# Attention over 64 graphs in even steps of one unit each, its probabilities transposed by DMA instead of TensorE

## What is computed

```
B, N, D, H = 64 graphs, 128 nodes, 512, 8 heads of 64
def attn(q, k, v, mask):
    scores = einsum('bhid,bhjd->bhij', q, k) * 64 ** -0.5
    w = softmax(where(mask > 0, scores, -inf))
    return einsum('bhij,bhjd->bhid', w, v)
edges = ln(attn(x @ wq1, x @ wk1, x @ wv1, adj.T) + x)          # pass 0
nodes = ln(attn(x @ wq2, edges @ wk2, edges @ wv2, adj) + x)    # pass 1
h = gelu(nodes @ w1 + b1)
out = layernorm(x + ln(nodes + h @ w2 + b2))
```

## Time and profile before

| | |
|---|---|
| time, median of 3 runs | 3141.88 us (3140.71 to 3142.14) |
| profiled execution, first to last instruction (span) | 3138.1 us |
| PE busy | 3028.9 us, 97% of the span |
| DVE, ACT, POOL busy | 56%, 45%, 48% of the span |
| DMA moved | 228.50 MB, mean 73 GB/s |
| TensorE clock granted, mean | 0.995 |

### The profile page before, as it was taken

One profiled execution on the slowest core, in us unless ns is written; L12 is line 12 of the kernel. 1 busy time (PEld: TensorE's weight loads), 2 busy tenths in 40 slices (PEclk: granted clock), 3 DMA queues, 4 the chain that ended last, 5 costly groups with the idle time before them and its releaser, 6 DMA issues.

```text
span 3138.1 us, 54583 instructions
## 1 busy us (share of the span) xinstructions
PE 3028.9 (97%) x18944; PEld 2511.9 (80%) x18944; DVE 1765.9 (56%) x4762; ACT 1422.4 (45%) x3754; POOL 1507.8 (48%) x1418
## 2 busy tenths in 40 slices
PE   8999999999899999999998999999999999999996
PEld 7888888888788888878887888888888888888885
DVE  6777777777787878777776233333232333332334
ACT  5656565656566666566665322222222222222221
POOL 3656564656466667676764233333323333332324
PEclk9999999999999999999999999999999999999998
DMA  4121212221223233333334311101111111001101
GB/s 155 59 74 60 71 61 71 64 75 59 81 92 115 98 114 99 112 101 111 100 108 134 99 54 54 43 18 53 53 47 53 53 53 53 27 33 53 54 34 60
DMA packets 167312, 228.50 MB, mean 73 GB/s; under 512 B 7168, under 2 KB 72832, under 8 KB 167168
## 3 DMA queue, kind: packets, MB, share of 16 engines
q1 hardware_dynamic: 167168, 226.86, 22.2%
HBM read 159.73 MB, written 67.11 MB: 72 GB/s over the span
## 4 chain that ended last, share of the span: by engine, by line
PE 84%; DVE 11%; issue 2%; ACT 2%; DMA 1%; SPq 0%; DVEq 0%; POOL 0%; POOLq 0%; ACTq 0%
PE proj L798 28%; PE proj L1278 22%; PE score L1292 11%; PE pt L1292 11%; PE score L847 4%; DVE normed L627 4%; PE att_out L874 3%; PE pt L856 2%; PE att_turn L782 2%; DVE att_pt_lo L691 1%; DVE att_probs L684 1%; DVE att_k_lo L668 1%; ACT att_q_hi L440 1%; ACT att_probs L446 1%; DVE att_k_lo L665 1%
## 5 line engine op out<-in xcount | busy, mean ns | idle before, releaser
L1222 DVE TENSOR_TENSOR hidden_lo<-hidden,hidden_hi 128x512 fp32r<-128x512 f32 x256 | 215.1, 840 | 954.6 <-ACT hidden_hi L1063 954.6
L1070 ACT ACTIVATE hidden<-proj,ffn_bias 128x512 f32<-128x512 f32 x256 | 176.2, 688 | 1021.4 <-PE proj L1278 1021.4
L446 ACT ACTIVATE att_probs<-att_probs,att_minus_max 128x128 f32<-128x128 f32 x1024 | 397.0, 390 | 198.9 <-DVE att_minus_max L684 198.9
L85 POOL TENSOR_TENSOR pool_scratch<-pool_scratch 128x1 f32<-128x1 f32 x144 | 27.8, 193 | 856.1 <-DVE ffn_moments L1166 491.6
L684 DVE CUSTOM_DVE_ANT_0 att_probs<-score,att_mask 128x128 f32<-128x128 f32 x1024 | 226.5, 285 | 27.6 <-issue 19.3
L798 PE MATMUL proj<-source_hi,weight_k_hi 128*128 128x512 f32 x512 | 214.9, 420 | 20.7 <-DVE att_k_lo L668 20.7
L691 DVE TENSOR_TENSOR att_pt_lo<-pt,att_pt_hi 128x512 f16<-128x512 f32 x256 | 175.1, 684 | 94.2 <-ACT att_pt_hi L451 94.2
L798 PE MATMUL proj<-weight_v_hi,source_hi 128*128 128x512 f32 x512 | 210.2, 410 | 11.7 <-DVE weight_v_lo L640 11.2
L580 POOL TENSOR_TENSOR source_lo<-source_raw,source_hi 128x512 fp32r<-128x512 f32 x128 | 167.9, 1333 | 91.2 <-ACT source_hi L471 91.1
L1278 PE MATMUL proj<-source_hi,w_lo 128*128 128x512 f32 x512 | 203.5, 397 | 0.0
L1278 PE MATMUL proj<-source_lo,w_hi 128*128 128x512 f32 x512 | 202.9, 396 | 0.0
(11 more groups left out here) (155 smaller groups left out, 9098.1 us busy)
## 6 DMA issues: line engine op xcount, KB each, us to landing
att_tokens<-in_x SPq DMA_DIRECT2D x32, 1024.0 KB, 5.5
source_raw<-in_x_t SPq DMA_DIRECT2D x16, 1024.0 KB, 5.8
edges_t<-turned SPq DMA_DIRECT2D x64, 256.0 KB, 2.3
source_raw<-edges_t SPq DMA_DIRECT2D x16, 1024.0 KB, 7.8
att_query_raw<-in_x_t SPq DMA_DIRECT2D x16, 1024.0 KB, 7.9
nodes_t<-turned SPq DMA_DIRECT2D x64, 256.0 KB, 2.3
nodes<-normed SPq DMA_DIRECT2D x16, 1024.0 KB, 5.7
source_raw<-nodes_t SPq DMA_DIRECT2D x16, 1024.0 KB, 7.6
```

The source lines that it names most:

```text
L446: nc.scalar.activation(probs[:, j, :], probs[:, j, :], ACT.Exp, bias=minus_max[:, j:j + 1], scale=-1.0, accum_out=row_sum[:, u % 2, j:j + ...
L1070: nc.scalar.activation(hidden[:, c % 2, :], up_bank[c % 2][:], ACT.Gelu, bias=bias_1[:, c:c + 1]).then_inc(activated, 1)
L1222: nc.vector.tensor_tensor(hidden_lo[:, c % 2, :], hidden[:, c % 2, :], hidden_hi[:, c % 2, :].bitcast(F32), ALU.subtract).then_inc(hidden_ ...
```

## The change

The work of a group is laid out in four even **steps**, one a unit. A step on PE is: key projection, query projection, `weigh` of the unit two before, one value projection, scores. The softmax of a unit falls into the step after its scores.

- The transposes on PE, their PSUM banks `pt_bank` and the casts out of them are gone. ACT rounds the probabilities to float16 in SBUF (`probabilities_high`), DVE takes the remainder (`probabilities_low`), and SP turns each half (four tiles) of each part by a DMA transpose of its own: four of 128 KB a step, each with its own semaphore (`turn_probabilities`). `weigh` waits for two of them before its first half and two before its second. There is one buffer `pt_hi`, `pt_lo`, so a step's transposes wait until `weigh` of the unit before is done.
- The freed banks go to the projections: four `proj_bank` in place of two.
- The residual sum and its statistics go unit by unit (`add_weighed`) on DVE; `centre` moves to ACT, which gets `offset` from POOL for it.
- SP loads the residual `tokens` in four parts of 256 KB instead of one of 1024 KB. All SP work (loads, stores, transposes) stands in one order, written out by hand.
- The last two units of the last group are weighed within the first feed-forward group. Otherwise feed-forward stays.

The diff, cut to its core (SP, then ACT, DVE, PE):

```diff
+    def turn_probabilities(sp, n):
+        wait(sp, weighed, n)
+        sp.sem_inc(sp_steps, 1)
+        for h in range(2):
+            half_of = slice(4 * h, 4 * h + 4)
+            sp.wait_ge(p_hi_ready, 2 * n + h + 1)
+            sp.sem_inc(sp_steps, 1)
+            sp.dma_start_transpose(pt_hi[:, half_of, :], p_hi[:, half_of, :].rearrange("p j i -> p (j i)")).then_inc(hi_turned[h], 16)
+            sp.wait_ge(p_lo_ready, 2 * n + h + 1)
+            sp.sem_inc(sp_steps, 1)
+            sp.dma_start_transpose(pt_lo[:, half_of, :], p_lo[:, half_of, :].rearrange("p j i -> p (j i)")).then_inc(lo_turned[h], 16)
...
+            if not starts(g):
+                turn_probabilities(sp, C * g - 1)
+            load_tokens(sp, g, own, 2)
+            turn_probabilities(sp, C * g)
+            load_tokens(sp, g, own, 3)
+            load_source(sp, g + 2, own)
+            turn_probabilities(sp, C * g + 1)
...
+            if not at(g, last_group - 1):
+                load_tokens(sp, g + 1, after, 0)
+            if not starts(g):
+                store_turned(sp, g - 1, before, 0)
+            turn_probabilities(sp, C * g + 2)
+            if not starts(g):
+                store_turned(sp, g - 1, before, 1)
+                store_turned(sp, g - 1, before, 2)
+                if before == 1:
+                    store_tokens(sp, g - 1, 1 - parity)
...
+    def centre(act, g, parity, b):
+        if b == 0:
+            act.wait_ge(offset_ready, g + 1)
+        data = total[parity][:, b, :]
+        nc.scalar.activation(data, data, ACT.Identity, bias=offset[:, b:b + 1], scale=rstd[:, b:b + 1]).then_inc(centred, 1)
...
-        def transposed_high(g, u, h):
-            act.wait_ge(pt_ready, 2 * (C * g + u) + h + 1)
-            nc.scalar.copy(pt_hi[:, 4 * h:4 * h + 4, :], pt_bank[h][:].rearrange("p (j i) -> p j i", j=4)).then_inc(pt_hi_ready, 1)
+        def probabilities_high(n, h):
+            wait(act, hi_turned[h], 16 * n)
+            act.wait_ge(exped, UNIT * n + 4 * h + 4)
+            nc.scalar.copy(p_hi[:, 4 * h:4 * h + 4, :], probs[:, 4 * h:4 * h + 4, :]).then_inc(p_hi_ready, 1)
...
-            nc.vector.tensor_tensor(pt_lo[:, 4 * h:4 * h + 4, :], pt_bank[h][:].rearrange("p (j i) -> p j i", j=4),
-                                    pt_hi[:, 4 * h:4 * h + 4, :], ALU.subtract).then_inc(pt_split, 1)
+        def probabilities_low(n, h):
+            wait(dve, lo_turned[h], 16 * n)
+            dve.wait_ge(p_hi_ready, 2 * n + h + 1)
+            nc.vector.tensor_tensor(p_lo[:, 4 * h:4 * h + 4, :], probs[:, 4 * h:4 * h + 4, :], p_hi[:, 4 * h:4 * h + 4, :],
+                                    ALU.subtract).then_inc(p_lo_ready, 1)
...
+            for u in range(C):
+                n = C * g + u - 1
...
+                    mask_and_maximum(n, g if u == 1 else None)
...
+                key_low(g, own, u)
...
+                query_low(g, own, u)
+                if not first:
+                    probabilities_low(n, 0)
+                    probabilities_low(n, 1)
+                if u < 2:
+                    if not starts(g):
+                        add_weighed(dve, g - 1, 1 - parity, before, u + 2)
+                    value_rest(g, parity, u + 2)
+                else:
+                    add_weighed(dve, g, parity, own, u - 2)
+                    if not at(g, last_group - 1):
+                        value_rest(g + 1, 1 - parity, u - 2)
...
+            for u in range(C):
+                turning = u == C - 1 and not starts(g)
+                keys(g, parity, own, u)
+                if turning:
+                    turn(pe, g - 1, 1 - parity, 0)
+                queries(g, parity, own, u)
+                if u >= 2:
+                    weigh(pe, g, parity, u - 2)
+                elif not starts(g):
+                    weigh(pe, g - 1, 1 - parity, u + 2)
+                if turning:
+                    turn(pe, g - 1, 1 - parity, 1)
+                if u < 2:
+                    values(g, parity, own, u + 2)
+                elif not at(g, last_group - 1):
+                    values(g + 1, 1 - parity, after, u - 2)
+                if turning:
+                    turn(pe, g - 1, 1 - parity, 2)
+                scores(g, u, 0)
+                if turning:
+                    turn(pe, g - 1, 1 - parity, 3)
+                scores(g, u, 1)
```

More of the change, by code:

```diff
@@ L222, in opens, with below, at @@
         return isinstance(group, int) and group % NG == 0 and group < last_group
+    def below(group, count):
+        return isinstance(group, int) and group < count
+    def at(group, value):
+        return isinstance(group, int) and group == value
     def over_passes(engine, body):
@@ L781, in turn, with weigh @@
         for c in range(C):
-            last = nc.tensor.transpose(turn_bank[:, c * P:(c + 1) * P], normed[:, b, c * P:(c + 1) * P], identity[:])
+            last = nc.tensor.transpose(turn_bank[:, c * P:(c + 1) * P], total[parity][:, b, c * P:(c + 1) * P], identity[:])
         last.then_inc(turned_ready, 1)
+    def weigh(pe, g, parity, u):
+        n = C * g + u
+        if u == 0:
+            pe.wait_ge(values_ready, GB * g + GB)
+        wait(pe, attended_ready, n)
+        for j in range(UNIT):
+            if j % 4 == 0:
+                pe.wait_ge(hi_turned[j // 4], 16 * (n + 1))
+                pe.wait_ge(lo_turned[j // 4], 16 * (n + 1))
+            b, column = j // 2, u * P + (j % 2) * HD
+            v = [part[:, b, column:column + HD] for part in v_part[parity]]
+            hi, lo = pt_hi[:, j, :], pt_lo[:, j, :]
+            out = out_bank[:, j * HD:(j + 1) * HD]
+            products = ((hi, v[0]), (hi, v[1]), (hi, v[2]), (lo, v[0]), (lo, v[1]))
+            for i, (p, value) in enumerate(products):
+                last = nc.tensor.matmul(out, p, value, start=(i == 0), stop=(i == len(products) - 1))
+        last.then_inc(weighed, 1)
     @block.tensor
@@ new lines, in scores @@
+            for i in range(2):
+                b = 2 * h + i
+                products = parts([q[:, b * P:(b + 1) * P] for q in (q_hi, q_lo)],
+                                 [k[:, :, b * P:(b + 1) * P] for k in (k_hi, k_lo)])
+                for n, (q, k) in enumerate(products):
+                    last = nc.tensor.matmul(
+                        score_bank[h][:, 2 * i * P:2 * (i + 1) * P].rearrange("p (s j) -> p s j", s=2), q, k,
+                        start=(n == 0), stop=(n == 2))
@@ L878, in body @@
+            last.then_inc(scored, 1)
+        values(0, 0, 0, 0)
+        values(0, 0, 0, 1)
         def body(g, parity, before, own, after):
             if ends(g):
[L880 to L883 removed]
                 return
[L885 to L887 removed]
@@ L1081, in body @@
                     attention["copy_turned"](act, c - TURNS)
+                if starts(g) and c == CENTRE:
+                    attention["centre"](act)
         over_groups(act, body)
@@ L1303, in body @@
                     down(g, c - 1)
+                if starts(g) and c in WEIGH:
+                    attention["weigh_last"](pe, 2 + WEIGH.index(c))
                 if c == 0 and not starts(g):
```

693 lines of the change are left out of this document (327 added, 366 removed).

## The result

The changed kernel takes 3170.05 us (median of 4 runs, 3168.5 to 3171.09) against 3141.3 us, 1.0093 times as long, 95% interval 1.0079 to 1.0107. The forecast was 3180, slower by 38 us; it became 29. The profiled execution's span is 3167.2 us against 3138.1, so it shows the same 29.

What follows compares the result with a forecast made beforehand. A loop through ACT and DVE in every step was taken as the bound: 11.7 + 14.6 + 12.8 + 13.9 = 53.0 us a group against 51.8, +1.2 x 32 = +38 us, 3180 us; range 3065 to 3300.

Steps and rivals of the forecast that it cites:

- The first step, 13.9: First step of a group, after the turning one: ACT's fourth copy waits for a store behind four transposes; 13.9 us.
- The hold: SP issuing one transposing DMA: taken as occupied 1.15 us, from the mask's copy, which also moves 512 pieces.
- some 3 us a group: Expected profile sign: ACT's fourth copy waiting some 3 us a group for the DMA into `edges_t`.
- The plain step, 11.7: Step without centring or turns: work of DVE and ACT closes a loop in 11.7 us, PE's 11.0 beside it.
- the two low parts, 1.86: DVE's low parts of probabilities, inputs in SBUF: 0.97 us each with POOL partly busy, two taken as 1.86.
- The third, 14.6: Step in which ACT centres: aggregates 0.8, two centrings 1.4, wait for POOL's `offset` 0.7, on 11.7: 14.6 us.
- The fourth, 12.8: Step that turns: one copy (0.46 us) behind ACT's exponentials and a wait at PE (0.6 us): 12.8 us.
- The 0.6 for PE's third turn: In the step that turns: PE's third turn, ahead of the scores, waits 0.6 us for ACT's second copy (estimate).
- Start, change of pass and hand-over at nothing, some 10 us: Kernel start, pass change and hand-over to feed-forward: costed at nothing; cover gone there could cost or bring some 10 us.
- The first (a hold like a plain copy's): A transpose holds SP no longer than a plain copy (0.39 us): 3110 us, 3036 with POOL leaving DVE alone; chance 0.29.
- The second, PE as the bound: PE remains the bound in attention at 45.7 us a group, -6.1 x 32: 2947 us; chance 0.03.
- The third (slow transfers in turn): Transposes slow on the transfer engines: 3470 us at 3 us each, some 4600 at 5.2; chance 0.09, with holds above 2.1.

## Why the prediction was right, and where it wasn't

- **The sign and the size** came out, 29 us against 38, but by luck and not by the sum. Without ACT's stops the change would have cost nothing that can be measured (3140.9 and 3140.0 against 3141): the sum alone was 38 us too high, and 29 us came from a cost that it didn't have. The range held both. The mechanism, a loop through ACT and DVE with two waits in it, was right.
- **The first step, 13.9:** measured 14.48. From the first transpose's issue to the store's it is 5.50 us where the sum had 4 x 1.25, which is most of the difference. The hold was taken at 1.15 from the mask's issue and is 1.20, but the reason given for it, the number of pieces, isn't what sets it: half and twice as many rows hold SP as long, and the mask's own copy took 0.39 in pass 0. So the near hit of this term is luck too. The wait for the store, "some 3 us a group", is 5.2. Moving the store showed that it is this wait.
- **The plain step, 11.7:** the loop alone, without aggregates, is 10.8 (the first step with the store moved). The term that failed most is the two low parts, 1.86 against 1.28. Their price, 0.97 each (two would be 1.94, not 1.86), lay on a line through POOL's mean share (on it POOL busy throughout would give 1.12, not 1.25), and a mean doesn't hold for a place: with POOL idle, two take 1.28, with its gain and shift beside them 2.55. The rest of the 0.9 I haven't split up. That the loop stands is shown by each step's first maximum, which starts as DVE's remainder ends while ACT waits for it, and by 123.8 us of idle time of the scores ended by q's low part.
- **The third, 14.6:** 14.55, from 10.8 for the loop, 1.1 for the offset (where I had 0.7), 1.4 for two centrings and 1.3 for the slowed low parts. Errors cancel here: the loop is 0.9 shorter, the aggregates (0.8) lie in the second step, the low parts take 1.3 more than in a plain step, the wait 0.4 more.
- **The fourth, 12.8:** 11.61, the loop and 0.8 for the copies: q's low part waits 2.05 us for ACT where a plain step has 1.58, and the first low part of the probabilities another 0.31. The 0.6 for PE's third turn doesn't show. This step (1.2 too high) and the plain one (0.3), less what the first was too low (0.6), are the 0.9 us a group (53.0 against 52.1), 29 us.
- **"Start, change of pass and hand-over at nothing, some 10 us":** without stops, in the run with the code shifted, a group is 0.2 us longer than before in pass 0 and 0.3 in pass 1, 6 us over the 26 groups between the second mask and the last but one of the two passes. From the last but one mask of all to the end it takes 1557.2 us against 1564.8 before, so it is given back at the end of attention and in feed-forward.
- **The step that was missing:** code. The trace before had the sign, which I passed over: its mask after a jump waits up to 2.6 us for "issue", five times, all in pass 0 (us in total, times, longest).

```profile
DVE att_mask L735 <- issue: 12.4, 5, 2.6
```

- **Rivals.** The first (a hold like a plain copy's) needed under 0.85 and falls with 1.20. With the store moved, the first step is the one that it describes, and the time of 3066 then lies between its 3110 and 3036. The second, PE as the bound, is reached only after two waits are gone. The third (slow transfers in turn) fails: a transfer lands 2.4 us after its issue, the next is issued 1.3 us after the one before, and PE never waits for them. The Trainium skill (VectorE: DVE Perf Modes, The three transpose paths) has 1309 ns for one 128x128 bf16 tile by DMA; four in turn would be an estimated 5.2 us. Here four tiles (128 KB) land in 2.4 us and eight (256 KB) in 3.2, so they overlap.

## What to carry to other kernels

A transfer that replaces work on an engine is paid for at the queue that issues it: ask what stands behind it there, and who waits for that; here one store put ahead of four transfers was worth 104 us, some 30 of them stops that it covered, where the change as a whole cost 29. Before a small loss is put down to a change, look for idle time with no releaser where a loop jumps back: here 96 instructions ahead of a loop moved the time by 30 us. Waits in different steps add up only until the next bound: two of 104 and 107 us gave 161 together.

## What was unexpected of the hardware

A transposing transfer of 64, 128 or 256 KB holds the issuing queue 1.2 us each, and lands in 2.3, 2.4 and 3.2 us: in this range size is almost free, the count isn't. DVE's low part of probabilities, all of it in SBUF, took half of 1.28 us alone and half of 2.55 with POOL's gain and shift beside it.

ACT's stop at a jump was 5.4 us in the changed kernel and gone with the code 96 instructions further on; DVE's were 2.3 us on average, in both passes, and ACT's with the store moved was at most 3.0. So place decides whether there is a stop, and something else how long it is. In the changed kernel no code arrives from ACT's copy (done at 1169.98) to 1173.6; with the store moved, where DVE jumps at the same moment, two packets come within 0.7 us of the copy (done at 1206.89). The transfer engines (last but one column, the share of their time) were full in the first case and not in the second:

```profile
1168.00:1175.00 7.00, 7.00 (x66) 5.58 (x64) 2.06 (x18) 0.59 (x1) 5.03 (x6) 1.00 1.05 328
...
1206.90:1209.90 3.00, 3.00 (x15) 2.46 (x14) 0.46 (x5) 0.00 (x0) 2.94 (x4) 1.00 0.59 135
```

That the fetch queues behind data there would fit, but no run changes this alone.

TensorE's clock fell after the long stop. The busy times of two short stretches there, the granted clock behind POOL's time:

```profile
1175.00:1181.00 6.00, 0.19 (x1) 0.00 (x0) 1.74 (x3) 5.51 (x20) 0.00 (x0) 0.72 0.53 170
1181.60:1185.00 3.40, 3.40 (x15) 3.31 (x16) 3.23 (x8) 1.68 (x4) 2.65 (x2) 0.57 0.38 77
```

PE stood idle for 6.4 us up to 1181.57, and the twelve scores after it followed each other at 0.21 us, in place of 0.12 elsewhere (the lower level, 1.2 GHz in place of 2.4); the projections from 1184.63 on were at full pace again. It cost little here, since DVE was busy with the low parts and the sum until 1185.8.
